# Six one-hot tiles of a counted block made by two comparisons of fp16 tensors on VectorE

## The reference, cut to what matters

```
scores = einsum('ehd,ehd->eh', q[src], k[dst])
smax = segment_max(scores, src, num_segments=N)
ex = exp(scores - smax[src])
denom = segment_sum(ex, src, num_segments=N)
attn = ex / denom[src]
out = segment_sum(attn[:, :, None] * v[dst], src, num_segments=N)
```

## Time and profile before

| | us |
|---|---|
| median of the 3 timed runs | 2411.66 |
| lowest and highest of them | 2403.01, 2413.3 |
| the profiled execution's own time | 2415.14 |
| its span in the profile | 2413.2 |
| busy TensorE (matmul) | 2363.5 |
| busy VectorE | 1412.7 |
| busy ScalarE | 962.9 |
| busy GpSimd | 923.0 |

### The profile page before, as it was taken

One profiled execution on the slowest core, in us unless ns is written; L12 is line 12 of the kernel. 1 busy time (PEld: TensorE's weight loads), 2 busy tenths in 40 slices (PEclk: granted clock), 3 DMA queues, 4 the chain that ended last, 5 costly groups with the idle time before them and its releaser, 6 DMA issues. The chain is left out here.

```text
span 2413.2 us, 27609 instructions
## 1 busy us (share of the span) xinstructions
PE 2363.5 (98%) x9345; PEld 1401.6 (58%) x9345; DVE 1412.7 (59%) x2944; ACT 962.9 (40%) x1663; POOL 923.0 (38%) x1271
## 2 busy tenths in 40 slices
PE   8999999999999999999999999999999999999998
PEld 4565655546677556577556577666567664543443
DVE  7897671432776653677554487555377555633435
ACT  5886643221665221466221276321166422212221
POOL 2005203030565330365341075452056543436674
PEclk9999999999999999999999999999999999999999
DMA  5401101230566310366310166510056601769417
GB/s 168 139 19 32 45 14 52 86 112 18 125 156 164 128 59 18 78 155 161 89 43 22 44 160 159 137 43 22 18 140 159 181 35 55 260 199 350 146 42 229
DMA packets 132171, 257.23 MB, mean 107 GB/s; under 512 B 49503, under 2 KB 51279, under 8 KB 129692
## 3 DMA queue, kind: packets, MB, share of 16 engines
q1 hardware_dynamic: 85102, 150.39, 21.3%
q0 software_dynamic: 45584, 102.75, 15.3%
q10 hardware_dynamic: 1346, 2.33, 0.3%
HBM read 212.95 MB, written 31.98 MB: 101 GB/s over the span
## 5 line engine op out<-in xcount | busy, mean ns | idle before, releaser
L114 POOL DMA_DIRECT2D cols<-w x720 | 354.0, 499 | 573.9 <-PE psum L655 338.6
L684 PE MATMUL psum<-cols,rows 128*128 128x256 f32 (+1 forms) x1600 | 369.2, 379 | 0.0
L670 PE MATMUL psum<-g_k_cols,g_q_cols 128*125 128x512 f32 (+1 forms) x960 | 360.6, 513 | 0.0
L684 PEld LDWEIGHTS psum<-cols,rows 128*128 128x128 f32 (+1 forms) x1600 | 303.3, 190 | 39.9 <-issue 4.2
L875 ACT ACTIVATE g_prob<-g_prob,g_row_max 125x1250 f32<-125x1250 f32 x160 | 214.0, 1337 | 239.2 <-DVE g_row_max L788 236.9
L788 DVE CUSTOM_DVE_ANT_0 g_prob<-psum,ln_count 125x1250 f32<-125x1250 f32 x160 | 233.5, 1459 | 105.4 <-PE psum L670 105.4
L670 PEld LDWEIGHTS psum<-g_k_cols,g_q_cols 128*125 128x125 f32 x960 | 179.4, 187 | 171.3 <-issue 163.0
L802 DVE STREAM_TRANSPOSE w<-g_prob 128x1280 f32<-128x1280 f32 x160 | 241.5, 1510 | 42.2 <-DMA cols<-w 24.0
L881 ACT ACTIVATE g_prob<-g_prob,g_row_max 125x1250 f32<-125x1250 f32 x160 | 214.1, 1338 | 107.3 <-DVE g_row_max L778 107.3
L2831 PE MATMUL psum<-m_ew,m_x_cols 128*64 128x256 f32 (+1 forms) x576 | 152.1, 495 | 1.4 <-DMA cols<-in_L_ffn_expert_w,m_weights_of 0.8
L741 PE MATMUL psum<-w,g_k_cols 128*125 128x512 f32 x320 | 143.6, 592 | 0.0
(11 more groups left out here) (395 smaller groups left out, 3948.9 us busy)
## 6 DMA issues: line engine op xcount, KB each, us to landing
cols<-w POOLq DMA_DIRECT2D x720, 80.0 KB, 3.2
cols<-w SPq DMA_DIRECT2D x560, 80.0 KB
w<-in_L_gnn_m_w SPq DMA_DIRECT2D x8, 1024.0 KB
slot_rows<-p_kf SPq DMA_DIRECT2D x1, 7128.0 KB, 32.6
rows<-slot_rows SPq DMA_DIRECT2D x54, 132.0 KB
m_ew<-in_L_ffn_expert_w SPq DMA_DIRECT2D x4, 1536.0 KB, 11.8
slot_outputs<-slot_rows SPq DMA_DIRECT2D x1, 5000.0 KB
w<-in_L_mix_W SPq DMA_DIRECT2D x4, 1024.0 KB, 5.2
```

The costliest lines, as they stand in the source:

```text
L114: return eng.dma_start(out, in_, allow_slow_non_contiguous=True)
L670: ins = pe.matmul(psum[0:P, at:at + width], q_cols[:, h, t * P:(t + 1) * P], k_cols[:, h, start:start + width], start=True, stop=True)
L684: ins = pe.matmul(c.bank(6 + g % 2, 256).rearrange("p (u a i) -> p u a i", u=2, a=SIDE), rows[0:r, j, h * 128:(h + 1) * 128], turned_keys[ ...
```

## The change

- VectorE always makes six tiles of a block (`HOT_DVE = W - 2`), and ScalarE always two; `dve_tiles` and `hots_before` are gone.
- VectorE makes its six tiles by two `tensor_tensor` comparisons of fp16 operands. One compares `iota[:, 0:128]`, taken again for each of the six tiles, with the source keys; the other `iota[:, 0:256]` with the second keys. A scalar operand can be only one key per partition, so the keys come as a tensor: `repeated` holds each key eight times (`SAME`), in fp16. The operands are read in rows of eight: eight numbers of `iota` against the eight copies of a key, and the same eight copies for all 16 or 32 rows of a tile.
- `repeat_keys_act(s)`, new, writes `repeated` for a set of 10 blocks: two ScalarE copies of 480 columns, from fp32 to fp16, in a buffer of two sets. It stands before ScalarE's tiles of block 0 (set 0), after those of block 1 (set 1), and behind blocks 12, 22 and 32 (sets 2, 3 and 4). VectorE waits for it at the first block of a set.
- The parts of a tile have 128 and 256 columns in place of 125 and 250. ScalarE makes them in that width. TensorE multiplies all 128 columns of the first part (128 rows of the sum in place of 125) and 250 of the second.
- TensorE waits for VectorE's six tiles at once, before the first, and then for each of ScalarE's.
- The semaphores of GpSimd's `iota` tables and of `sets` are one, `tables_made`; the instructions and their order stay.

The diff, cut to its core:

```diff
+    HOT_DVE, SAME = W - 2, 8
+    SRC_COLS, KEY_COLS = 128, 256
+    SET_BLOCKS = BLOCKS // SETS
...
-        iota = sb("iota", [P, KEYS], F16)
+        iota = sb("iota", [P, KEY_COLS], F16)
...
-        def dve_tiles(b):
-
-            return W - 2 if b % 3 == 2 else W - 1
...
+        def repeat_keys_act(s_):
+
+            s = c.act
+            if s_ == 0:
+                s.wait_ge(keys_copied, 2)
+            if s_ >= 2:
+                s.wait_ge(hot_made, 2 * SET_BLOCKS * (s_ - 1))
+            of = slice(s_ * SET_ROWS, (s_ + 1) * SET_ROWS)
+            for n in range(2):
+                s.copy(repeated[:, s_ % 2, n].rearrange("p b (k c) -> p b k c", c=SAME),
+                       edge_cols[:, n, of].rearrange("p (b k) -> p b k", k=W)[:, :, 0:HOT_DVE].unsqueeze(3).broadcast_to(
+                           [P, SET_BLOCKS, HOT_DVE, SAME])).then_inc(keys_repeated, 1)
 
         def hot_dve(b):
             v = c.dve
+            s_, at = divmod(b, SET_BLOCKS)
+            if at == 0:
+                v.wait_ge(keys_repeated, 2 * (s_ + 1))
             if b >= 2:
                 v.wait_ge(summed, b - 1)
-            for k in range(dve_tiles(b)):
-                hot = hots[:, b % 2, k, :]
-                e = b * W + k
-                v.tensor_scalar(hot[:, 0:P], iota[:, 0:P], edge_cols[:, 0, e:e + 1], None, ALU.is_equal).then_inc(
-                    hot_made, 1)
-                v.tensor_scalar(hot[:, P:], iota[:, :], edge_cols[:, 1, e:e + 1], None, ALU.is_equal).then_inc(hot_made, 1)
+            for n, (c0, width) in enumerate(((0, SRC_COLS), (SRC_COLS, KEY_COLS))):
+                shape = [P, HOT_DVE, width // SAME, SAME]
+                v.tensor_tensor(hots[:, b % 2, 0:HOT_DVE, c0:c0 + width].rearrange("p k (j c) -> p k j c", c=SAME),
+                                iota[:, 0:width].rearrange("p (j c) -> p j c", c=SAME).unsqueeze(1).broadcast_to(shape),
+                                repeated[:, s_ % 2, n, at].rearrange("p (k c) -> p k c", c=SAME).unsqueeze(2).broadcast_to(shape),
+                                ALU.is_equal).then_inc(hot_made, 1)
...
-            for k in range(dve_tiles(b), W):
-                hot = hots[:, b % 2, k, :]
-                for n, part in enumerate((hot[:, 0:P], hot[:, P:])):
-                    s.activation(part, iota[:, 0:(P, KEYS)[n]], ACT.Abs,
-                                 bias=away_cols[:, n, b, k - W + 2:k - W + 3]).then_inc(hot_apart, 1)
+            for k in range(W - HOT_DVE):
+                hot = hots[:, b % 2, HOT_DVE + k, :]
+                for n, part in enumerate((hot[:, 0:SRC_COLS], hot[:, SRC_COLS:])):
+                    s.activation(part, iota[:, 0:(SRC_COLS, KEY_COLS)[n]], ACT.Abs,
+                                 bias=away_cols[:, n, b, k:k + 1]).then_inc(hot_apart, 1)
...
+            pe.wait_ge(hot_made, 2 * (b + 1))
             for k in range(W):
-                if k < dve_tiles(b):
-                    pe.wait_ge(hot_made, 2 * (hots_before(b) + k + 1))
-                else:
-                    pe.wait_ge(hot_act_made, W * b - hots_before(b) + k - dve_tiles(b) + 1)
+                if k >= HOT_DVE:
+                    pe.wait_ge(hot_act_made, (W - HOT_DVE) * b + k - HOT_DVE + 1)
                 hot = hots[:, b % 2, k, :]
-                ins = pe.matmul(c.bank(6 + b % 2, KEYS, P), hot[:, 0:P], hot[:, P:], start=(k == 0), stop=(k == W - 1))
+                ins = pe.matmul(c.bank(6 + b % 2, KEYS), hot[:, 0:SRC_COLS], hot[:, SRC_COLS:SRC_COLS + KEYS],
+                                start=(k == 0), stop=(k == W - 1))
...
+                    if b % SET_BLOCKS == 2 and b // SET_BLOCKS + 1 in range(2, SETS):
+                        repeat_keys_act(b // SET_BLOCKS + 1)
...
                 if t == NT - 2:
+                    repeat_keys_act(0)
                     s.wait_ge(away_made, 1)
                     hot_act(0)
             hot_act(1)
+            repeat_keys_act(1)
```

More of the change, by code:

```diff
@@ L999, in performer @@
     z_cond, z_scaled, z_made, z_turned, y_made = c.sems("p_z_cond", "p_z_scaled", "p_z_made", "p_z_turned", "p_y_made")
-    ident_made, iotas_made, sets_made = c.sems("ident_made", "iotas_made", "sets_made")
+    ident_made, tables_made = c.sems("ident_made", "tables_made")
     dst_in, const_step, consts_made, opens_made = c.sems("dst_in", "const_step", "consts_made", "opens_made")
@@ L1007, in performer @@
                                                                            "hot_act_made", "summed", "counted")
+    keys_repeated = c.sem("keys_repeated")
     next_sent, next_made, ends_turned = c.sems("next_sent", "next_made", "ends_turned")
@@ L1088, in performer @@
         qf_cols = shared[:, 0:2 * 4 * 2 * P].rearrange("p (u e a n) -> p u e a n", u=2, e=2, a=2)
-        hots = shared[0:P, 0:W * (P + KEYS)].bitcast(F16).rearrange("p (u k n) -> p u k n", u=2, n=P + KEYS)
+        HOT = SRC_COLS + KEY_COLS
+        hots = shared[0:P, 0:W * HOT].bitcast(F16).rearrange("p (u k n) -> p u k n", u=2, n=HOT)
+        repeated = shared[0:P, W * HOT:W * HOT + 2 * SET_BLOCKS * HOT_DVE * SAME].bitcast(F16).rearrange(
+            "p (u n b f) -> p u n b f", u=2, n=2, b=SET_BLOCKS)
         none = shared[0:P, 0:2 * N].rearrange("p (u n) -> p u n", u=2)
@@ L1264, in pool_start @@
                     (freq[0:FREQ, 0:1], [[0, 1]], 1, 1), (freq[FREQ:2 * FREQ, 0:1], [[0, 1]], 1, 1),
-                    (iota[:], [[1, KEYS]], 0, 0))):
+                    (iota[:], [[1, KEY_COLS]], 0, 0))):
                 if n >= 1:
-                    g.wait_ge(iotas_made, n)
+                    g.wait_ge(tables_made, n)
                 g.iota(out, pattern, base=base, channel_multiplier=per,
[L1269 to L1272, removed]
+                       allow_small_or_imprecise_dtypes=True).then_inc(tables_made, 1)
+            g.wait_ge(tables_made, 8)
+            g.memset(sets[:], 1.0).then_inc(tables_made, 1)
+            g.wait_ge(tables_made, 9)
             g.affine_select(out=sets[:], in_=sets[:], compare_op=ALU.is_ge, fill=0.0, base=0,
-                            pattern=[[1, SETS * SET_ROWS]], channel_multiplier=-W).then_inc(sets_made, 1)
-            g.wait_ge(sets_made, 2)
+                            pattern=[[1, SETS * SET_ROWS]], channel_multiplier=-W).then_inc(tables_made, 1)
+            g.wait_ge(tables_made, 10)
             g.affine_select(out=sets[:], in_=sets[:], compare_op=ALU.is_ge, fill=0.0, base=W - 1,
-                            pattern=[[-1, SETS * SET_ROWS]], channel_multiplier=W).then_inc(sets_made, 1)
+                            pattern=[[-1, SETS * SET_ROWS]], channel_multiplier=W).then_inc(tables_made, 1)
             g.wait_ge(rows_made, 1)
@@ L1298, in start_dve @@
             v.memset(ones[:], 1.0).then_inc(ones_made, 1)
-            v.wait_ge(iotas_made, 2)
+            v.wait_ge(tables_made, 2)
             v.tensor_scalar(row[:, 1:2], row[:, 0:1], 1.0 / W, -(W - 1) / (2.0 * W), ALU.mult, ALU.add).then_inc(
@@ L1315, in start_dve @@
             v.wait_ge(consts_made, 3)
-            v.wait_ge(iotas_made, 5)
+            v.wait_ge(tables_made, 5)
             v.wait_ge(dst_in, 16)
@@ L1333, in start_dve @@
                                    ALU.mult).then_inc(opens_made, 1)
-            v.wait_ge(iotas_made, 7)
+            v.wait_ge(tables_made, 7)
             v.tensor_scalar(freq[:, 0:1], freq[:, 0:1], 1.0 / 16.0, None, ALU.mult).then_inc(freq_made, 1)
@@ L1425, in sets_pe @@
             pe = c.pe
-            pe.wait_ge(sets_made, 3)
+            pe.wait_ge(tables_made, 11)
             pe.wait_ge(first_made, 2)
@@ L1615, in keys_dve @@
             v = c.dve
-            v.wait_ge(iotas_made, 8)
+            v.wait_ge(tables_made, 8)
             v.wait_ge(gathered, 16 * 2 * SETS)
@@ L1677, in hot_act @@
                 s.wait_ge(summed, b - 1)
-            made = W * b - hots_before(b)
-            for k in range(dve_tiles(b), W):
-                hot = hots[:, b % 2, k, :]
-                for n, part in enumerate((hot[:, 0:P], hot[:, P:])):
-                    s.activation(part, iota[:, 0:(P, KEYS)[n]], ACT.Abs,
-                                 bias=away_cols[:, n, b, k - W + 2:k - W + 3]).then_inc(hot_apart, 1)
-            for k in range(dve_tiles(b), W):
-                hot = hots[:, b % 2, k, :]
-                made += 1
+            for k in range(W - HOT_DVE):
[3 more added lines that the diff above has]
+                                 bias=away_cols[:, n, b, k:k + 1]).then_inc(hot_apart, 1)
+            for k in range(W - HOT_DVE):
+                hot = hots[:, b % 2, HOT_DVE + k, :]
+                made = (W - HOT_DVE) * b + k + 1
                 s.wait_ge(hot_apart, 2 * made)
@@ L1988, in count_tile @@
             for n in range(N // KEYS):
-                v.tensor_scalar(dst_hot[:, n * KEYS:(n + 1) * KEYS], iota[:, :], cur_dst[:, n:n + 1], None,
+                v.tensor_scalar(dst_hot[:, n * KEYS:(n + 1) * KEYS], iota[:, 0:KEYS], cur_dst[:, n:n + 1], None,
```

2 lines of the change are left out of this document (removed).

## The result

| | before | after |
|---|---|---|
| median, us | 2407.66 (9 runs) | 2416.29 (9 runs) |
| lowest and highest | 2402.33, 2413.3 | 2411.24, 2419.83 |
| profiled execution: time, span | 2415.14, 2413.2 | 2417.69, 2416.0 |

The ratio is 1.0044, with a 95% interval of 1.0032 to 1.0056: slower by 8.6 us, a little inside the 0.5% that the prediction took as its bound, with an interval that reaches over it. (The ratio is not the quotient of the two medians, which is 1.0036: 0.44% would be 10.6 us.

The account below looks back on a forecast made before the run. VectorE was taken to pace much of the counting, ScalarE after the change: 37.4 us of new ScalarE work less 26.0 of room, plus 0.4 and 0.5 unfilled, gives +12.3 on 2411.66, so 2424.0 us; range 2414 to 2438.

Parts of the forecast that it names:

- Those named for "right": In the counting: ScalarE busy over 19 us per 20 from 80 to 190, few waits, TensorE awaiting Relu, last count near 201.
- signs named for "wrong": In the counting: ScalarE waiting 10 us or more, TensorE waiting for new comparisons, or granted clock under 1.00 before 190 us.
- (a): ScalarE's counting: 34 of 50 blocks go from one ScalarE tile to two, adding 31.6 us.
- (b): ScalarE's tiles: they widen from 125, 250 and 375 to 128, 256 and 384 columns, adding 1.4 us.
- (c): ScalarE's new key repeating: ten copies of 480 columns at 0.44 us add 4.4 us, bounds 2.5 to 8.8.
- ScalarE's room: ScalarE's idle time in the counting: 22.1 us in 39 waits plus 3.9 of overlap, 26.0 us for new work.
- I carry all of it: From the last count to the kernel's end: the whole 12.3 us delay reaches the end, since TensorE is nearly full.
- the end does not depend on this choice: VectorE's comparisons: whichever column price holds, even 2.93 us a block, 147 us fits under ScalarE's 149.
- The first, the clock: TensorE idles while ScalarE paces and its clock falls to 1.2 GHz: +5 us for one fall, about 2429; chance 0.08.
- The second (fine-grained operands): VectorE's rows of eight cost over 1.18 ns a column, so VectorE paces; 2450 at 3.5 us a block; chance 0.06.
- The third (faster): In the counting, VectorE was the bound and ScalarE absorbs the new tiles, TensorE's 9.9 us wait goes: 2402; chance 0.05.
- The fourth (the delay is taken up later): After the counting, a transfer hidden anyway takes up the delay and the time stays near 2412; chance 0.03.

Follow-up runs that it names:

- experiments 1 to 4: The kernel before with six tiles on VectorE, then the changed kernel with seven, eight, or tripled repeating copies: 2414.28, 2401.43, 2400.89 and 2435.22 us, in that order.
- Experiment 1: The kernel before, scalar comparisons kept, but always six tiles of a block on VectorE and two on ScalarE: 2414.28 us, ratio 1.0022.
- experiments 1, 2 and 4: The kernel before with six tiles on VectorE, the changed kernel with seven, and with repeating copies made three times: 2414.28, 2401.43 and 2435.22 us.
- experiment 5: The changed kernel with repeated keys in fp32, four times each: 2422.48 us, ratio 1.0054 to the kernel before.
- experiment 4: The changed kernel with each pair of ScalarE's repeating copies made three times, with waits between the pairs: 2435.22 us, ratio 1.0107 to the kernel before.
- experiment 8: The changed kernel with each key repeated two or four times in place of eight: 2422.10 and 2423.97 us, one run each.
- halves: The seven-tile kernel with each comparison cut into four tiles and three, TensorE waiting for each part separately: 2400.24 us, ratio 0.9958 to the kernel before.

## Why the prediction was right

**What paces.** The prediction said that ScalarE would take over the pace from VectorE, and that the kind of comparison would not matter. The waits, experiments 1 to 4 and the 20.00 us of 20 on ScalarE show it. Experiment 1 alone, with no new comparison in it, has most of the loss.

**The signs.** Those named for "right" came: ScalarE was busy for over 19 us in each 20 from 80 to 160, its waits shrank from 22.1 to 2.4 us, TensorE waits for its Relu, and the last copies of counts start at 200.09. But from 160 to 180 us ScalarE was busy for 18.32 only, and two of the signs named for "wrong" came too: a granted clock under 1.00 before 190 us (0.74 and 0.50), and TensorE waiting for the new comparisons, 3.1 us. Both were small here, and ScalarE lost no more than its 2.4 us of waiting by them.

**The terms.** (a) The second tile: a two-tile block was put at 2.44 + 0.03 us and takes 2.46. (b) was right with it. (c) A repeating copy was put at 0.44 us (its own terms, 0.25 and 230 columns at 0.77 ns, give 0.43) and holds ScalarE for 0.49: ten of them 4.9 us, not 4.4. That is what the Trainium skill ("ScalarE: Activation LUTs", What ACT_TABLE_LOAD costs) had given as the estimate; the row's 592 ns agrees with its 586. ScalarE's room was put at 26.0 us, all but 0.9 of it to be filled. Sum +12.3; the stretch grew by 10.8 us where ScalarE never waited and by 13.6 where it waited 2.4 us. The sum was for the whole kernel, though, and there the timed difference is 8.6.

**The number.** 2424.0 us is 7.7 over the measured 2416.29. Of this 4.0 is the base: the median of the kernel before was 2411.66 us in three runs and is 2407.66 in nine. The other 3.7 is the difference, 12.3 forecast and 8.6 measured.

**Where these 3.7 us go stays open.** The step in question is "I carry all of it". In every kernel the timed difference to before lies under that of the stretch, by 1.6 us (experiments 1, 2 and 4) to 3.5 (experiment 5), for the changed kernel by 2 to 5. The profiles show how far the delay gets. At TensorE's first instruction on the experts' gathered rows (start, us, of the kernel before and of the changed one; first profiles) it is whole:

```profile
2127.67 0.66 PE L2816 MATMUL psum<-ident,rows 128*128 128x128 f32 x4 [1.30 <-DMA rows<-slot_rows]
```

```profile
2140.65 1.11 PE L2835 MATMUL psum<-ident,rows 128*128 128x128 f32 x4 [2.35 <-DMA rows<-slot_rows]
```

That is 13.0 us of delay here and 16.3 in the second profiles (2126.08 and 2142.34). From the first feature matmul to this point takes 1936.5 to 1941.4 us in all twelve profiles. The rest, to the end of the span, takes 273.1 to 285.5 us, with no order by kernel: 285.5 and 279.2 before, 275.3 and 280.2 after. At the end of the span the changed kernel is 2.8 us late in the first pair and 17.2 in the second. So most of the scatter lies in the last 280 us, and whether these also take up some of the delay can't be told from it.

**VectorE.** Its block was put at 2.63 us, with 0.95 to 2.93 as bounds, and takes 1.34 (two instructions span 1.43 us, four 2.77). The step that failed is the choice of the fp32 row as the nearest: from the shortest comparison of 768 columns, 546 ns, to the 951 of 1536 the slope is 0.53 ns a column, half of the fp32 row's 1.03. The Trainium skill ("VectorE: DVE Perf Modes", the perf-mode tier table) has it right, two results a cycle for tensor_tensor of 16-bit operands. It did not enter the sum, as said. Experiment 5 runs VectorE at nearly the rate of the prediction's value, and the stretch is about 6 us longer for it, so "the end does not depend on this choice" was too strong by that: with the 2.63 us that the prediction took, the loss would have been some 6 us larger in the stretch.

**The rivals.** The first, the clock, came about in small. It was priced at 5 us for a fall; two falls cost 2.4 us of ScalarE's waiting here, five cost 6.1 in experiment 4. The price was too high because a projection at half speed is partly hidden by the two or three blocks that ScalarE has still to make: the one of 6.16 us from 165.85 cost ScalarE 1.5 us. The second (fine-grained operands) needed over 1.18 ns a column and is refuted by the 0.53 of the changed kernel, whose operands come in rows of eight; experiment 8 finds the same with rows of four and two. The third (faster) is refuted by the result: it needed two-tile blocks of 2.0 us, and they take 2.46. That the kernel with one tile on ScalarE comes to 2401.43 us, near this rival's 2402, is a coincidence of the base. The fourth (the delay is taken up later) is refuted up to 2127 us, as shown above, and open for the last 280.

**The chances.** The forecast sat on the 0.5% bound; the result is 0.44%, or 0.36% by the medians. "Slower" had 0.53 and "within" 0.42, and it is "within" that came, narrowly: the interval goes from 0.32 to 0.56%. The rows could not tell the two apart.

## What to carry to other kernels

When a change speeds one engine up and moves a little work to another, add up the other engine's work against its idle time in that stretch first: here 37 us of new work met 26 us of room, and no gain on VectorE could make up for it. Three nearly full engines have to be balanced by the longest one, and the split is cheap to move: one tile per block back to VectorE turned +8.6 us into -6.1. Those 6.1 us are about what the faster comparison is worth, for the kernel before had nearly the same split (seven tiles on VectorE in two of three blocks). Where the consumer waits for a group of results, cut the group so that it can start on the first part: TensorE's wait for the comparisons fell from 6.3 to 2.6 us, and the stretch by 2.2.

## What was not expected of the hardware

- Loading 128 columns of fp16 weights takes 98 ns where 125 columns took 136 (LDWEIGHTS of the sums, L1716 against L1702). The tiles' pitch went from 375 to 384 elements with the width, and no run tells the two apart. The matmuls of 250 columns between them hide both: their median is 270 ns in either kernel.

```profile
L1716 PEld LDWEIGHTS psum<-p_shared x400: 94/98/106, 55.1 to 199.9; 125*128 125x128 f16 x134
```

- While GpSimd's one multiplication ran (2.38 us from 78.27 in the kernel before), a scalar comparison of VectorE that takes 0.25 us took 2.44. The comparison of two tensors is held as well: one of 768 columns took 2.74 us in place of 0.60, from 79.53 us, beside GpSimd's multiplication from 78.93 (second row, of the changed kernel: shortest, median, longest in ns).

```profile
78.27 2.44 DVE L1669 TENSOR_SCALAR p_shared<-iota,p_edge_sum 125x125 f16<-125x125 f16 x1
```

```profile
L1684 DVE TENSOR_TENSOR p_shared<-iota,p_shared x100: 546/945/2737, 51.6 to 195.1; 125x768 f16<-125x768 f16 x50, 125x1536 f16<-125x1536 f16 x50
```

- TensorE's clock fell in every kernel in which ScalarE paced, one to five times in the stretch: once in experiment 1, twice and once in the two profiles of the changed kernel, twice in each kernel of experiment 8, five times in experiment 4. In experiment 5 it fell four times, three of them after TensorE had waited for VectorE. It did not fall in the stretch of the kernel before, nor with seven tiles, eight or halves; in some of these it fell right behind the counting.
